# Six result places and shorter rows of scattered transfers in a mixture of experts, and a scan's first decays made one chunk earlier

## The chip, the cores and the metric

The kernel runs on one core of one Trainium2 chip. The metric is device time in microseconds (us), the median of three runs. The profiled execution of the kernel before lasted 853.98 us, of which its instructions span 852.2 us.

## The reference

Two sequences of 1,024 tokens with 128 features go through six residual layers: a small FFN, an attention, the FFN again, a mixture of experts, a bidirectional Mamba-2 layer, and the same mixture of experts again. The change touches the last three.

```python
x = x + 0.5 * ffn(layernorm(x));  x = x + attention(layernorm(x));  x = x + 0.5 * ffn(layernorm(x))
x = x + 0.5 * experts(layernorm(x))      # 8 experts, top 2, at most 320 tokens of a sequence in each
x = x + mamba_bidirectional(layernorm(x))
x = x + 0.5 * experts(layernorm(x))

def experts(h):                           # per sequence, e in 8 experts
    p = softmax(h @ gate.T); pick 2; keep the first 320 tokens of an expert
    y[e] = (silu(h[e] @ w1[e]) * (h[e] @ w3[e])) @ w2[e]          # 320x128, 128x448, 448x128
    out[token] += p[token, e] * y[e]

def mamba(u):                             # each direction
    z, xBC, dt = split(u @ Wi.T); xBC = silu(conv4(xBC) + b); dt = softplus(dt + bias)
    h = h * exp(dt * A) + dt * x * B;  y = h @ C + D * x          # a scan over 1,024 tokens
    return rmsnorm(y * silu(z)) * norm_w @ Wo.T
```

## The kernel before

**Experts.** A unit is one sequence's one expert: units 0 to 15 are the first layer of experts (HALF = 16), 16 to 31 the second. Rows of x are scattered to memory by expert (`scatter`, an indirect DMA of POOL for 128 rows; a routing has 8 or 16 of them). SP loads a unit's 320 rows (`load`, a ring of three), PE turns them (`turn`), and four chunks of hidden features (FCH = 4) follow: `hidden` on PE, `silu` on ACT, `gating` on DVE. `gating` counts the semaphore `gated`, one per chunk over all units, so gated 91 is chunk 2 of unit 22. PE makes the results, ACT keeps them, PE turns them back, and ACT weighs them (`weigh`) into one of OUT places in SBUF, two or so units later. POOL then sends the place to memory by token (`send`, three indirect DMAs a unit, each followed by its landing on `y_out` of the place). `weigh` waits until the last unit in its place has landed. SENT_AT tells for which unit POOL waits for which count of `gated` before it sends, and so how its transfers lie in time; all of POOL's work is one queue in program order. When a sequence's eight units have landed, SP fetches its rows (`fetch`) and DVE adds them to x (`combine`). `address` on DVE makes a unit's row numbers and weights.

**Where the Mamba layer begins.** Beside units 10 to 15 the first sequence is combined and normalised, turned, its step sizes are made (`steps` on PE, `step_sizes` on DVE, `exp_dt` on ACT), and the first direction is projected (`project`, `take`, `first_tap`, `convolve`).

**Scan.** 32 chunks g of 128 tokens, eight (NC) for each of four units of direction and sequence. For a chunk, PE's `before(g)` makes transposes and a product; ACT's `exps(g)` makes the decays between positions: four Relu (L2124), a copy of `bs` (L2129), and one Exp (L2131); DVE's `front(g)` makes `xdt`, `gm` and, with the decays, `mt`; PE's `outputs(g)` and DVE's `back(g)` end it. Each step g of the loops starts chunk g + 1 ahead: `before(g + 1)`, `exps(g + 1)`, `front(g + 1)`. In step 6 of a unit (GATES_AT) ACT also takes both z pieces of the next unit with Silu and makes the four Silu of its convolved rows (`silu_rows`); only then can PE's `before` of the next unit's first chunk begin. In steps 6 and 7 of the first and third scan unit the normalisations for the layers after stand on the same queues.

## Time and profile before

| | us |
|---|---|
| three runs, median (lowest, highest) | 852.98 (852.75, 858.59) |
| profiled execution, its time | 853.98 |
| span of its instructions | 852.2 |
| FFN and attention, first part | 0 to 320 |
| first experts, units 0 to 15 | 320 to 484 |
| scan | 499 to 690 |
| second experts, units 16 to 31, from the end of the scan | 690 to 852 |

Times in the rows are counted from the first instruction. A line number (L1690) is one of the kernel before. The idle time in brackets is that of the engine before the instruction, with what released it; "remote" is a release that the profile can't put down to one instruction. Matmul ends are modelled, and a few per cent of records can be missing.

### The profile page before, as it was taken

How to read it: one execution, taken by the hardware profiler on the slowest of the kernel's cores; microseconds unless marked ns; L12 is line 12 of the kernel's file. 1: busy time of each engine (PE TensorE's matmuls, PEld its weight loads, DVE VectorE, ACT ScalarE, POOL GpSimd, SP SyncE). 2: the span in 40 equal slices, each digit the busy share in tenths (PEclk: the TensorE clock that was granted, in tenths of full speed). 3: DMA queues.
4: the chain of work that ended last, by engine and by line, in shares of the span. 5: the costliest groups of instructions: out<-in, count | busy, mean ns of one | idle time of the engine just before them, and what ended most of it. 6: DMA issues, size and time to landing. Idle time of an engine off the chain costs nothing. (4 is left out here: it accounts for less than half of the span.)

```text
span 852.2 us, 12981 instructions
## 1 busy us (share of the span) xinstructions
PE 716.2 (84%) x4016; PEld 373.4 (44%) x4016; DVE 496.4 (58%) x1453; ACT 543.8 (64%) x938; POOL 298.8 (35%) x328
## 2 busy tenths in 40 slices
PE   4799999989999997898779886778887768797995
PEld 1432222212222224565446454566566645564654
DVE  6778432204855747743437469798798847332352
ACT  5367997889998983644256684967877615342331
POOL 3090003301000434434323456444562732545342
PEclk9799999999999999999889988998999979998998
DMA  4046934521492211112212042112221311211313
GB/s 130 1 187 161 183 86 81 199 91 60 175 261 82 86 36 50 40 34 50 80 28 55 20 117 56 58 50 60 71 72 52 99 49 56 58 42 47 88 53 89
DMA packets 76410, 70.11 MB, mean 82 GB/s; under 512 B 9687, under 2 KB 60233, under 8 KB 76080
## 3 DMA queue, kind: packets, MB, share of 16 engines
q1 hardware_dynamic: 71024, 60.56, 26.6%
q0 software_dynamic: 5024, 8.54, 3.0%
q8 instruction: 36, 0.59, 0.3%
q14 instruction: 38, 0.31, 0.1%
q10 hardware_dynamic: 288, 0.10, 0.1%
HBM read 41.23 MB, written 29.02 MB: 82 GB/s over the span
## 5 line engine op out<-in xcount | busy, mean ns | idle before, releaser
L687 ACT ACTIVATE attn_p<-attn_ps 128x1024 f32<-128x1024 f32 x256 | 240.7, 1059 | 34.7 <-PE attn_ps L703 20.7
L1665 PE MATMUL ps_main<-moe_xsT,moe_w 128*128 128x320 f32 x384 | 131.0, 469 | 14.6 <-issue 9.1
L703 PE MATMUL attn_ps<-attn_p,attn_v 128*32 128x512 f32 x1024 | 137.5, 608 | 4.2 <-issue 4.0
L1675 ACT ACTIVATE moe_act_h<-ps_main 128x320 f32<-128x320 f32 (+1 forms) x128 | 55.1, 433 | 115.2 <-PE ps_main L1665 60.6
L1690 DVE TENSOR_TENSOR moe_hid<-moe_act_h,ps_main 128x320 f32<-128x320 f32 (+1 forms) x128 | 61.9, 485 | 110.8 <-ACT moe_act_h L1675 51.0
L1559 POOL DMA_INDIRECT moe_slots<-rows,moe_scatter_at x64 | 63.8, 997 | 97.8 <-DVE moe_scatter_at L1548 38.0
L680 PE MATMUL attn_ps<-attn_q_rows,attn_k_rows 64*128 64x512 bf16 x448 | 84.5, 388 | 11.5 <-ACT attn_p L687 7.7
L1665 PEld LDWEIGHTS ps_main<-moe_xsT,moe_w 128*128 128x128 f32 x384 | 70.7, 200 | 49.7 <-issue 29.5
L1695 PE MATMUL ps_main<-moe_hid,moe_w 128*128 128x320 f32 (+1 forms) x256 | 74.9, 458 | 5.1 <-DVE moe_hid L1690 3.7
L680 PEld LDWEIGHTS attn_ps<-attn_q_rows,attn_k_rows 64*128 64x128 bf16 x448 | 20.3, 93 | 134.2 <-ACT attn_p L687 119.6
L1765 POOL DMA_INDIRECT moe_rows<-moe_y,moe_dest x48 | 46.2, 962 | 78.6 <-ACT moe_y L1758 39.7
L2084 DVE SCALAR_TENSOR_TENSOR mb_act<-mb_padded,mb_taps,mb_act 128x1024 f32<-128x1024 f32 x48 | 67.1, 1407 | 2.9 <-ACT mb_act L2075 2.3
L1695 PEld LDWEIGHTS ps_main<-moe_hid,moe_w 128*128 128x128 f32 (+1 forms) x256 | 41.9, 192 | 34.7 <-issue 15.3
L1195 POOL TENSOR_TENSOR x_sb<-x_sb,bout_half 128x1024 f32<-128x1024 f32 (+1 forms) x4 | 7.3, 1837 | 104.7 <-DVE rows L1150 104.7
L2245 POOL TENSOR_TENSOR mb_z<-mb_y_in,mb_z 128x256 f32<-128x256 f32 x24 | 26.3, 1098 | 47.8 <-DVE mb_y_in L2236 33.0
L436 POOL TENSOR_SCALAR attn_parts<-attn_q 128x512 bf16<-128x512 f32 x4 | 2.5, 616 | 114.6 <-DVE attn_q L398 114.6
L2124 ACT ACTIVATE mb_e_seg<-mb_cums,mb_cum_col 128x128 f32<-128x128 f32 x128 | 40.5, 389 | 1.2 <-DMA mb_cums<-mb_cum_kept 1.2
L703 PEld LDWEIGHTS attn_ps<-attn_p,attn_v 128*32 128x32 f32 x1024 | 20.6, 108 | 42.5 <-issue 36.9
L2048 PE MATMUL ps_side<-norm_xT,mb_w_xbc 128*128 128x512 f32 x64 | 33.4, 641 | 5.5 <-DVE mb_ab L2017 5.5
L1765 POOL DMA_INDIRECT moe_rows<-mb_y,moe_dest x24 | 22.9, 955 | 38.8 <-ACT mb_y L1758 24.8
L2179 PE MATMUL ps_main<-mb_xw,mb_bs 128*128 128x256 f32 x56 | 20.0, 442 | 19.6 <-DVE mb_h L2202 12.8
L2156 DVE TENSOR_TENSOR mb_mt<-mb_e_seg,mb_gm 128x512 f32<-128x512 f32 x32 | 26.9, 840 | 15.6 <-ACT mb_e_seg L2131 9.5
(273 smaller groups left out, 1288.0 us busy)
## 6 DMA issues: line engine op xcount, KB each, us to landing
mb_cums<-mb_cum_kept SPq DMA_DIRECT2D x32, 256.0 KB
moe_slots<-zeros SPq DMA_DIRECT2D x4, 1380.0 KB, 14.0
attn_q_rows<-attn_q_parts SPq DMA_DIRECT2D x36, 128.0 KB
attn_k_rows<-attn_k_parts SPq DMA_DIRECT2D x36, 128.0 KB
moe_w<-in_w SPq DMA_DIRECT2D x3, 1536.0 KB, 11.6
moe_rows<-zeros SPq DMA_DIRECT2D x4, 1024.0 KB, 16.2
moe_back<-moe_rows SPq DMA_DIRECT2D x16, 256.0 KB, 4.0
mb_e_cum<-mb_e_cum_kept SPq DMA_DIRECT2D x56, 64.0 KB
```

The lines of the kernel that those rows point to most:

```text
L680: ins = self.core.nc.tensor.matmul(into, self.k_rows[rows, ring, pair, keys], self.q_rows[rows, ring, pair, queries], start=True, stop=True)
L687: self.core.nc.scalar.activation(self.p[:, w % self.PB, :, :].rearrange("p a n -> p (a n)"), self.ps_s[:, w % self.SB, :, :].rearrange("p ...
L703: ins = self.core.nc.tensor.matmul(self.ps_av[32 * i:32 * i + 32, :], self.v[:, b * TPB + kt, HGROUPS * i + m, :], self.p[:, w % self.PB, ...
L1559: nc.gpsimd.indirect_dma_start(self.slots[r], bass.IndirectOffsetOnAxis(self.scatter_at[:, b, k, j:j + 1], 0), self.row_of[:, b * TPB + j, ...
L1665: self.core.nc.tensor.matmul(ps[:, w % 2, 0:CAP], wt[:, e, c * P:(c + 1) * P], self.xsT[:, u % 2, :], start=True, stop=True).then_inc(self ...
L1675: self.core.nc.scalar.activation(self.act_h[into, w % 2, :], self.ps_h1[rows, w % 2, 0:CAP], ACT.Silu).then_inc(self.silu_done, 1)
L1690: self.core.nc.vector.tensor_tensor(self.hid[rows, u % 2, c, :], self.act_h[rows, w % 2, :], bank[rows, w % 2, 0:CAP], ALU.mult)\
L1695: return self.core.nc.tensor.matmul(self.y_bank(u)[:, 0:CAP], self.w2[rows, u % E_, c, :], self.hid[rows, u % 2, c, :], start=start, stop= ...
L1765: self.core.nc.gpsimd.indirect_dma_start(self.rows[u // E_], bass.IndirectOffsetOnAxis(self.dest[0:n, u % self.DEST, s:s + 1], 0), self.y[ ...
L2048: self.core.nc.tensor.matmul(bank[:], weight, self.xT[:, t0:t0 + BANK], start=True, stop=True).then_inc(self.proj_done, 1)
L2084: ins = self.core.nc.vector.scalar_tensor_tensor(out, src, tap, out, ALU.mult, ALU.add)
L2124: ins = nc.scalar.activation(self.e_seg[:, g % 2, hh, :], self.cums[:, g % 2, hh, :], ACT.Relu, bias=self.cum[:, di, n, hh:hh + 1], scale= ...
```

## The change

Six things are changed; the renaming of semaphores (`chain` and `sent` become one `addressed`, `dt_exp` and `a_exped` one `exped`) pays for two more `y_out`.

- OUT is 6 in place of 4: places 4 and 5 are lent from tiles of the scan (`y2`'s second part and `y_in`). At the start of the scan `back(0)` and `back(1)` on DVE and the third step of ACT wait for the landing of the units in these places.
- POOL's order in the first experts: the second routing is no longer scattered in one row of eight between units 1 and 2, but in two rows of four between units 3 and 4, which wait for gated 25 and 29. Units 2 and 3 are sent ahead of it without a wait; units 4 and 6 wait for 33 and 37 (they waited for 33 and 38).
- POOL's order in the second experts: both routings in rows of four, the last three of which wait for gated 79, 83 and 86; then five rows of six, two units each, that wait for 91, 96, 101, 106 and 111 (before: two rows of eight, and waits at 87, 94 and 99, the rest sent as soon as weighed).
- The first sequence's `combine`, normalisation, `steps`, `step_sizes`, `exp_dt` and `sums` beside units 10 to 13 stand two chunks to one unit later; `project` 0 and its `take` move from the end of unit 11 into unit 12.
- `exps` is split into `lower`, `keep_b` and `exp_lowered`. For the first chunk of scan units 1 to 3, `lower` and `exp_lowered` run one step earlier on ACT: in step 6, behind `exps` of the last chunk, and ahead of the z pieces and `silu_rows`.
- At the end, `add_last` of a half stands behind `combine` of the same half, not behind both.

```diff
-    OUT, DEST = 4, 8
+    OUT, DEST = 6, 8
...
-        SENT_AT = {2: FCH * 6 + 5, 4: FCH * 8 + 1, 6: FCH * 9 + 2,
-                   HALF: FCH * (HALF + 5) + 3, HALF + 2: FCH * (HALF + 7) + 2, HALF + 4: FCH * (HALF + 8) + 3}
+        SENT_AT = {4: 33, 6: 37, HALF: FCH * HALF + 27, HALF + 2: FCH * HALF + 32, HALF + 4: FCH * HALF + 37, HALF + 6: FCH * HALF + 42, HALF + 8: FCH * HALF + 47}
...
                 for u in range(HALF):
-                    if u == 2:
-                        moe.scatter(pool, 2)
+                    if u == 4:
+                        for n in (0, 4):
+                            pool.wait_ge(moe.gated, FCH * 6 + 1 + n)
+                            moe.scatter(pool, 2, n, n + 4)
                     if u in SENT_AT:
                         pool.wait_ge(moe.gated, SENT_AT[u])
                     moe.send(pool, u)
...
                     if u == HALF:
-                        moe.scatter(pool, 4)
-                        pool.wait_ge(moe.gated, FCH * (HALF + 3) + 2)
-                        moe.scatter(pool, 5)
+                        moe.scatter(pool, 4, 0, 4)
+                        for q, n, at in ((4, 4, 15), (5, 0, 19), (5, 4, 22)):
+                            pool.wait_ge(moe.gated, FCH * HALF + at)
+                            moe.scatter(pool, q, n, n + 4)
...
     def exps(self, act, g):
+        ahead = g >= self.NC and g % self.NC == 0
+        if not ahead:
+            self.lower(act, g)
+        self.keep_b(act, g)
+        if not ahead:
+            self.exp_lowered(act, g)
...
                     if g + 1 < N:
                         mamba.exps(act, g + 1)
+                    if u + 1 < UNITS and i == NC - 2:
+                        mamba.lower(act, g + 2)
+                        mamba.exp_lowered(act, g + 2)
...
-                        if u == 10 and c in (1, 2):
-                            moe.combine(dve, ch, 0, c - 1)
-                            norm.stats_of(dve, ch, c + 15)
+                        if (u, c) in ((10, 3), (11, 0)):
+                            moe.combine(dve, ch, 0, u - 10)
+                            norm.stats_of(dve, ch, u + 6)
...
-                        if u == 11 and c == 3:
+                        if u == 12 and c == 1:
                             mamba.exp_dt(act, 0)
+                        if u == 12 and c == 2:
+                            mamba.take(act, 0, 0)
+                            mamba.first_tap(act, 0, 0)
...
                 for half in range(2):
                     moe.combine(dve, ch, 3, half)
-                for half in range(2):
                     moe.add_last(dve, half)
```

## Rows read from the trace of the kernel before

**Rows 1.** Table by stretch: stretch, its us, busy us by engine, clock, DMA.

```profile
core 0: us, PE busy (x) PEld busy (x) DVE busy (x) ACT busy (x) POOL busy (x), PEclk, DMA share, GB/s
...
499.00:690.00 191.00, 149.79 (x1002) 113.06 (x999) 163.81 (x386) 137.81 (x306) 106.91 (x121) 0.94 0.24 67
...
716.00:852.00 136.00, 112.89 (x467) 72.19 (x465) 50.40 (x159) 46.22 (x123) 59.09 (x61) 0.94 0.24 66
```

**Rows 2.** Order of time, DVE: first gating of units 18, 20, 22, 24, 26.

```profile
716.48 0.49 DVE L1690 TENSOR_TENSOR moe_hid<-moe_act_h,ps_main 128x320 f32<-128x320 f32 x1 [0.69 <-PE ps_main L1665]
...
735.98 0.49 DVE L1690 TENSOR_TENSOR moe_hid<-moe_act_h,ps_main 128x320 f32<-128x320 f32 x1
...
751.55 0.49 DVE L1690 TENSOR_TENSOR moe_hid<-moe_act_h,ps_main 128x320 f32<-128x320 f32 x1
...
765.74 0.49 DVE L1690 TENSOR_TENSOR moe_hid<-moe_act_h,ps_main 128x320 f32<-128x320 f32 x1
...
787.73 0.49 DVE L1690 TENSOR_TENSOR moe_hid<-moe_act_h,ps_main 128x320 f32<-128x320 f32 x1 [0.90 <-PE ps_main L1665]
```

**Rows 3.** Order of time, POOL, second experts: indirect transfers, ends of four rows.

```profile
718.82 0.99 POOL L1559 DMA_INDIRECT moe_slots<-rows,moe_scatter_at  x1 [27.50 <-DVE moe_scatter_at L1548]
...
727.76 0.97 POOL L1559 DMA_INDIRECT moe_slots<-rows,moe_scatter_at  x1 [0.30 <-issue]
...
761.51 0.97 POOL L1765 DMA_INDIRECT moe_rows<-mb_y,moe_dest  x1 [3.84 <-DVE moe_hid L1690]
...
769.97 0.97 POOL L1765 DMA_INDIRECT moe_rows<-moe_y,moe_dest  x1 [1.21 <-issue]
...
780.06 0.91 POOL L1765 DMA_INDIRECT moe_rows<-mb_y,moe_dest  x1 [0.30 <-issue]
```

**Rows 4.** Waits by pair from 300 us on: us in total, times, longest.

```profile
ACT moe_act_h L1675 <- remote: 15.5, 3, 6.4
```

**Rows 5.** Order of time, PE and ACT, unit 19.

```profile
726.93 1.78 PE L1695 MATMUL ps_main<-moe_hid,moe_w 128*128 128x320 f32 x6
...
730.26 0.44 ACT L1675 ACTIVATE moe_act_h<-ps_main 128x320 f32<-128x320 f32 x1 [5.24 <-remote]
```

**Rows 6.** Order of time, POOL, first experts: starts of two rows of transfers.

```profile
399.56 0.97 POOL L1765 DMA_INDIRECT moe_rows<-moe_y,moe_dest  x1 [6.24 <-DVE moe_hid L1690]
...
429.82 0.97 POOL L1765 DMA_INDIRECT moe_rows<-moe_y,moe_dest  x1 [15.44 <-ACT moe_y L1758]
```

**Rows 7.** Order of time, DVE, units 9 and 11.

```profile
410.92 0.49 DVE L1603 COPY moe_xsT<-ps_main 128x320 f32<-128x320 f32 x1 [5.82 <-remote]
...
438.59 0.23 DVE L2015 TENSOR_TENSOR mb_v<-ps_side,mb_dt_bias 128x64 f32<-128x64 f32 x1 [4.48 <-remote]
```

**Rows 8.** Order of time, ACT, scan steps 6 and 7.

```profile
537.29 4.26 ACT L2091 ACTIVATE mb_act<-mb_act,mb_conv_b 128x1024 f32<-128x1024 f32 x4
...
542.71 1.27 ACT L2124 ACTIVATE mb_e_seg<-mb_cums,mb_cum_col 128x128 f32<-128x128 f32 x4
...
544.15 1.28 ACT L2131 ACT_TABLE_LOAD   x1
545.45 0.63 ACT L2131 ACTIVATE mb_e_seg<-mb_e_seg 128x512 f32<-128x512 f32 x1
```

**Rows 9.** Order of time, DVE, at the ends of the three scan units.

```profile
546.11 0.69 DVE L2156 TENSOR_TENSOR mb_mt<-mb_e_seg,mb_gm 128x512 f32<-128x512 f32 x1 [3.06 <-ACT mb_e_seg L2131]
...
549.23 0.70 DVE L2156 TENSOR_TENSOR mb_mt<-mb_e_seg,mb_gm 128x512 f32<-128x512 f32 x1 [1.11 <-ACT mb_e_seg L2131]
...
599.76 0.69 DVE L2156 TENSOR_TENSOR mb_mt<-mb_e_seg,mb_gm 128x512 f32<-128x512 f32 x1 [3.19 <-ACT mb_e_seg L2131]
...
643.55 0.18 DVE L1144 RECIPROCAL norm_rstd<-norm_std 128x4 f32<-128x4 f32 x1 [1.01 <-ACT norm_std L1115]
```

**Rows 10.** Order of time, SP: the fetch of the third sequence's rows.

```profile
790.86 2.01 SPq L1779 DMA_DIRECT2D moe_back<-moe_rows  x4
```

**Rows 11.** Order of time, DVE, the end.

```profile
845.94 0.69 DVE L1786 TENSOR_TENSOR x_sb<-x_sb,moe_back 128x512 f32<-128x512 f32 x1 [0.37 <-DMA moe_back<-moe_rows]
...
847.49 1.48 DVE L1649 TENSOR_TENSOR x_sb<-x_sb,ps_side 128x512 f32<-128x512 f32 x2
```

More of the change, by code:

```diff
@@ L1439, in open @@
         self.act_h, self.hid = sb("act_h", [P, 2, CAP]), sb("hid", [P, 2, FCH, CAP])
-        own = sb("y", [P, self.OUT // 2, 3, D])
-        self.y = [own[:, i, :, :] for i in range(self.OUT // 2)]
+        own = sb("y", [P, 2, 3, D])
+        self.y = [own[:, i, :, :] for i in range(2)]
         self.second = sb("second", [P, 2, 3])
@@ L1449, in open, with landed_of @@
         self.y_kept, self.y_turned = sem("y_kept"), sem("y_turned")
-        self.chain = sem("chain")
+        self.addressed = sem("addressed")
         self.y_out = [sem(f"y_out{i}") for i in range(self.OUT)]
         self.back_in = [sem(f"back_in{i}") for i in range(2)]
-        (self.turned, self.t_read, self.h_done, self.silu_done, self.gated, self.y_done, self.y_read, self.sent, self.combined) = (
-            sem(n) for n in ("turned", "t_read", "h_done", "silu_done", "gated", "y_done", "y_read", "sent", "combined"))
-    OUT, DEST = 4, 8
+        (self.turned, self.t_read, self.h_done, self.silu_done, self.gated, self.y_done, self.y_read, self.combined) = (
+            sem(n) for n in ("turned", "t_read", "h_done", "silu_done", "gated", "y_done", "y_read", "combined"))
+    OUT, DEST = 6, 8
+    def landed_of(self, place, unit):
+        return 48 * len([u for u in range(min(unit, self.LAST)) if u % self.OUT == place])
     UNITS = 2 * B * E_
@@ L2387, in _ @@
                             moe.counts(pe, 2)
-                        if u == 11 and c == 1:
+                        if u == 11 and c == 3:
                             norm.turn(pe, 16)
                             norm.turn(pe, 17)
-                        if u == 13 and c == 0:
+                        if u == 12 and c == 0:
+                            pe.wait_ge(norm.ready, 18)
+                            mamba.steps(pe, 0)
+                        if u == 12 and c == 1:
+                            mamba.project(pe, 0, 0)
+                        if u == 13 and c == 2:
                             mamba.sums(pe, 0)
```

77 lines of the change are left out of this document (40 added, 37 removed).

## The prediction

> **What bounds the kernel now.** I began with the table by stretch, since the change touches three stages with different limits. In the second experts PE is busy for 112.89 of 136.00 us while DVE, ACT and POOL are each under half; in the scan DVE leads with 163.81 of 191.00, ACT follows with 137.81. The granted clock is 0.94 in both, near the upper level, 2.4 GHz [rows 1]. So the experts can win only where PE stands still, and the scan where DVE or its supplier ACT does.
>
> To see whether PE stands still I went to DVE's order of time and read the first `gating` of every second unit. The pairs take 735.98 - 716.48 = 19.50, then 15.57, 14.19 and 21.99 us for the same work [rows 2]. The pair of 14.19 is the plain one; the others are 5.31, 1.38 and 7.80 longer.
>
> What lies beside the long pairs shows in POOL's order of time. Transfers of 0.97 with 0.30 of issue between them stand in rows without a break: eight from 718.82 to 728.73, six from 761.51, and, only 1.21 after these, nine from 769.97 to 780.97 [rows 3]. The plain pair holds the start of the row of six; the worst pair holds the nine that follow it. The list of waits then says what was late: ACT's `silu` waited three times, 15.5 in all and up to 6.4, for a release that the profile can't put to an instruction [rows 4]. One place shows it: PE's matmuls of unit 19 end at 728.71, no later work of PE is needed, and ACT starts at 730.26 after 5.24 idle [rows 5]. The eight transfers ended at 728.73. I read this as PE's progress reaching the others late while a long row runs. In the first experts the same view gives a row that begins at 399.56, and one at 429.82 [rows 6], and DVE stood still for 5.82 and 4.48 inside them [rows 7]. That rows and stalls belong together is a coincidence seen five times, not a proof: the row of eight before 751.55 cost at most 1.38, and the six at 761.51 nothing.
>
> In the scan, ACT's and DVE's orders of time around a change of unit are read together: ACT makes `silu_rows` (four of 4.26), Relu (four of 1.27), loads a table (1.28) and makes Exp (0.63) [rows 8]; DVE's `mt` waits for that Exp, 3.06 and 3.19 at the first two changes, and 1.11 for the next chunk's [rows 9].
>
> **The second experts.** Six places alone remove nothing that I can find: no long wait of `weigh` for a landing is seen, so what they allow is later and shorter rows. First what there is to remove: 1.38 of the second pair and 7.80 of the fourth go in whole. Of the first pair's 5.31, ACT's idle after PE's end is 1.55 and the rest is also routing work, so its stall lies between 1.55 and 5.31; I take 3.6, near the middle. Sum 12.8 (10.7 to 14.5) [rows 2, 5].
>
> What the new rows cost: three rows of four at 79, 83 and 86 behind a first one, and five of six at gated 91, 96, 101, 106 and 111. A chunk of the plain pair takes 14.19 / 8 = 1.77, so five take 8.87; six transfers take 6 x 1.27 = 7.6. A gap of 1.2 to 1.3 is left. A row of six cost nothing at 761.51; the row of six at 429.82 has 4.48 of waiting in it [rows 3, 6, 7]. So five rows cost 0 to 22; I take 1 each, near the row of the same stage, and nothing for rows of four, shorter than any that stalled. Gain 12.8 - 5 = 7.8.
>
> The later sends have a cost behind them: units 22 and 23 wait for gated 106, the second chunk of unit 26, and `fetch` of their sequence stands on SP ahead of the `load` of a later unit. It was issued at 790.86 and took 2.01 [rows 10]. With units some 8 us earlier and the fetch hardly so, the load may be late by 0 to 2.01; I take 0.6, since the ring holds three units. Net -7.2.
>
> The Trainium skill speaks against this. The page "DMA: Bandwidth & Descriptors", in "Issuing engines are not separate DMA queues", says that transfers started by different engines run on the same 16 DMA engines and interleave, so who starts them matters little. By that the same transfers at other times would cost the same, and the 7.8 would be none; the idle of 5.24 does not decide it, as it shows a delay and not its carrier [rows 5].
>
> **The first experts.** The row at 399.56 (twelve transfers) stays, with its waits one count apart. `steps` and `exp_dt` move away from the row at 429.82, where DVE's `step_sizes` had waited 4.48 [rows 6, 7]. Their instructions are the same and stand one chunk to one unit later, with PE's `project` behind them. This saves 0 to 4.48; I take 3.7, since the idle belongs to the wait and units go on beside it. Against this, sends 2 and 3 and the second routing in two fours become nearly one row of fourteen, where before a shorter one did: the nearest prices are 1.38 for eight and 5.82 for twelve, from which I take 1.7 (0 to 5.82), as the fours wait for counts. The `load` of unit 8 has its scatter later, and waits if that lands after unit 7; its margin is small, and its price is inside this range. Net -2.0 (-4.5 to +5.8). The two new waits for places at the start of the scan are for units 10 and 11, sent ahead of 14 and 15, for which the kernel waits there already: nothing.
>
> **The scan.** Three changes of unit. What moves: four Relu (1.27) and one Exp (0.63) of the next unit's first chunk, 1.9 of ACT, from behind `silu_rows` to ahead of it. No instruction and no table load is saved: after the Silu, the next Exp, now that of the second chunk, must load 1.28 [rows 8]. So it is a reordering on an engine that is busy without a break over the change. What wins: `mt` of the first chunk needn't wait for Exp, 3.06 and 3.19 [rows 9]. What loses: the z pieces and `silu_rows` come 1.9 later, so PE's `before` of that chunk, which needs them, comes 1.9 later, and DVE's `gm` behind that. ACT then waits for PE with `keep_b`, where before it made Relu and Exp; behind it in ACT's queue stand the second chunk's Relu and Exp, for whose predecessor DVE waited already (1.11). At the third change DVE waits for a normalisation's root (1.01), which stands behind the moved work, too. Each change can lose 1.9 + 1.28 = 3.2 and gain up to 3.2. I take +2.5, +0.5 and +2.5, nearer the loss, since the shared supplier ACT has no slack there; the second change is the one without normalisations beside it. Sum +5.5 (-3 to +9.6).
>
> The page "ScalarE: Activation LUTs" of the Trainium skill, in "What ACT_TABLE_LOAD costs", adds a drain of about 1.38 us to each load. By it a load exposed at three places would cost up to 4.1 more; in the rows here Exp follows its load within 0.02 us, so I leave it out.
>
> **The tail.** `add_last` of the first half moves ahead of `combine` of the second, which had waited 0.37 for its data; two `add_last` took 1.48 [rows 11]. One of them, 0.74, leaves the end as far as that wait covers it, and the first half is stored sooner: -0.5 (0 to -0.74).
>
> **The sum.** -7.2 - 2.0 + 5.5 - 0.5 = -4.2, from the profiled 853.98: 849.8. That execution is 1.0 above the median of the runs, 852.98; so 848.8, told as 848.5.
>
> **The rivals.** *Rows free, scan free* (838). If no row of six stalls, the second experts give 12.8 - 0.6 = 12.2; if ACT's order gives as much as it takes, the scan gives 0. With -2.0 and -0.5 this is 853.98 - 14.7 - 1.0 = 838.3. For it: the row of six at 761.51 cost nothing, and DVE's waits for Exp are long [rows 2, 3, 9]. Against it: 4.48 beside another row of six [rows 7].
>
> *Gaps too short* (slower, 861). If 1.2 us between rows doesn't let PE's progress through, the five rows of six are one row of thirty. The fifteen transfers from 761.51 to 780.97, parted by 1.21, cost 7.80, 0.52 each [rows 2, 3]: thirty cost 15.6 in place of 12.8, +2.8. With 0.6 for the fetch, the first experts at 0, +5.5 and -0.5 this is 853.98 + 8.4 - 1.0 = 861.4. It decides at the break that ends a row: above 1.2 us my forecast holds. For it: exactly such a break stood ahead of the worst pair. Against: its second row had nine.
>
> *No effect of rows* (858). The change doesn't do what it says: the stalls come with the traffic, which is the same, and not with how it is cut. Then the experts stay, and +5.5 - 0.5 is left: 853.98 + 5.0 - 1.0 = 858. For it: two rows of eight cost so differently. This is where the rule on the 16 engines would lead, too.
>
> **How the numbers follow.** The forecast has 0.50; by its terms' bounds its own range is 843 to 854, and a sixth of it, 0.08, lies below 844.5. Rows and scan free: 0.27. Gaps too short: 0.13, of which half is above 861.5. No effect of rows: 0.10. One per cent of 853, 8.5 us, is about what a measurement of this kernel can tell from no change. Faster by more than that (below 844.5): 0.27 + 0.08 = 0.35; slower (above 861.5): 0.06; the rest, 0.59. The range leaves out the lower third of the free case, 0.09, and some two thirds of the slow one, 0.09: 837 to 860.
>
> **What would show it.** Second experts: pairs of units near 14.2 to 16, no row of POOL above six, ACT's remote waits well under 15.5 in sum. If gaps are too short, the pairs from gated 91 on are near 18, with remote waits at ends of rows of six. First experts: no remote wait of 4 before `step_sizes`; the row at about 400 still stalls. Scan: `mt` of a first chunk without a wait for Exp, but `silu_rows` and PE's `before` 1.9 later, a table load ahead of the second chunk's Exp, and the scan 191 + 5.5 long. If it is 191 or shorter, the loss of ACT's order was wrong; if a row of six has a stall of 4, so was its price of 1.

## The result

The changed kernel takes 873.56 us (median of four runs, 871.1 to 881.02) against 852.87 of the kernel before: 1.0224 times, with a 95% interval of 1.0177 to 1.027. It is slower by some 20 us, outside the range of the prediction. Measured again later, the same pair gave 1.0243 (1.0188 to 1.0298). Ratios are of fast runs alone, slow ones left out, so a ratio can differ from that of two medians. The profiled execution of the changed kernel spans 879.2 us, 27.0 more than that of before.

Both kernels cut at the same points, the first `gating` of units 0, 15, 16 and 31 and the first and last `y_in` of the scan, show where the 27.0 lie:

| stage, us | before | after | difference |
|---|---|---|---|
| up to unit 0 | 329.9 | 329.0 | -0.9 |
| first experts, unit 0 to 15 | 144.2 | 153.3 | +9.0 |
| unit 15 to the scan | 25.1 | 24.4 | -0.6 |
| scan, first to last `y_in` | 187.7 | 199.3 | +11.6 |
| scan to unit 16 | 12.2 | 10.4 | -1.7 |
| second experts, unit 16 to 31 | 129.8 | 138.7 | +8.9 |
| from unit 31 on | 23.3 | 24.1 | +0.8 |

All three changed stages lost in this execution. It is the slowest of the four, 7.5 above their median. In a second profiled one (`after_again`, span 867.5) the scan lost 9.6 and the first experts 6.7, but the second experts 0.6 only. So the first two losses are of the kernel, and the third is mostly of this one execution. The table by stretch of the changed kernel, for the scan and the second experts, answers to [rows 1] (stretch, its us, busy us by engine, clock, DMA):

```profile
core 0: us, PE busy (x) PEld busy (x) DVE busy (x) ACT busy (x) POOL busy (x), PEclk, DMA share, GB/s
507.00:706.00 199.00, 159.19 (x996) 119.22 (x994) 162.24 (x376) 138.01 (x305) 105.97 (x119) 0.89 0.21 63
732.00:879.00 147.00, 124.72 (x474) 79.43 (x473) 53.04 (x181) 47.01 (x125) 59.19 (x61) 0.88 0.21 61
```

DVE, ACT and POOL are busy for as long as before. PE is busy longer, with the same matmuls, and its clock fell from 0.94 to 0.89 and 0.88: more of the time is at the lower of its two levels, 1.2 GHz. So the loss is waiting, and matmuls at half speed beside the waits.

**Second experts.** DVE's order of time, the first `gating` of units 18, 20, 22, 24 and 26, as in [rows 2], with the first of unit 25 and the other three of unit 26:

```profile
736.41 0.49 DVE L1696 TENSOR_TENSOR moe_hid<-moe_act_h,ps_main 128x320 f32<-128x320 f32 x1 [1.87 <-PE ps_main L1671]
...
755.12 0.49 DVE L1696 TENSOR_TENSOR moe_hid<-moe_act_h,ps_main 128x320 f32<-128x320 f32 x1
...
770.99 0.49 DVE L1696 TENSOR_TENSOR moe_hid<-moe_act_h,ps_main 128x320 f32<-128x320 f32 x1
...
788.52 0.49 DVE L1696 TENSOR_TENSOR moe_hid<-moe_act_h,ps_main 128x320 f32<-128x320 f32 x1 [0.55 <-PE ps_main L1671]
...
797.64 0.49 DVE L1696 TENSOR_TENSOR moe_hid<-moe_act_h,ps_main 128x320 f32<-128x320 f32 x1 [1.77 <-ACT moe_act_h L1681]
...
802.89 0.49 DVE L1696 TENSOR_TENSOR moe_hid<-moe_act_h,ps_main 128x320 f32<-128x320 f32 x1
804.12 0.49 DVE L1696 TENSOR_TENSOR moe_hid<-moe_act_h,ps_main 128x320 f32<-128x320 f32 x1 [0.74 <-ACT moe_act_h L1681]
806.16 0.49 DVE L1696 TENSOR_TENSOR moe_hid<-moe_act_h,ps_main 128x320 f32<-128x320 f32 x1 [1.15 <-PE ps_main L1671]
816.48 0.49 DVE L1696 TENSOR_TENSOR moe_hid<-moe_act_h,ps_main 64x320 f32<-64x320 f32 x1 [9.83 <-ACT moe_act_h L1681]
```

The pairs take 18.71, 15.87, 17.53 and 14.37. The bad place has moved: in unit 26 there are 10.32 between two gatings that are neighbours (806.16 and 816.48). POOL's order of time, as [rows 3], says why:

```profile
798.90 0.97 POOL L1771 DMA_INDIRECT moe_rows<-mb_y,moe_dest  x1 [3.25 <-DVE moe_hid L1696]
...
805.23 0.91 POOL L1771 DMA_INDIRECT moe_rows<-mb_y_old,moe_dest  x1 [0.30 <-issue]
806.45 0.97 POOL L1771 DMA_INDIRECT moe_rows<-mb_y,moe_dest  x1 [0.30 <-issue]
...
812.77 0.91 POOL L1771 DMA_INDIRECT moe_rows<-mb_y_in,moe_dest  x1 [0.30 <-issue]
```

The row of six for gated 101 begins at 798.90. The counts 101 and 106 came 6.48 apart (the gatings of 797.64 and 804.12), in less than the 7.6 that six transfers take. So the next six followed with no break: a row of twelve. ACT's order of time, and under it the list of waits, which answer to [rows 5] and [rows 4]:

```profile
816.02 0.43 ACT L1681 ACTIVATE moe_act_h<-ps_main 64x320 f32<-64x320 f32 x1 [7.34 <-remote]
```

```profile
ACT moe_act_h L1681 <- remote: 23.2, 3, 11.2
```

`silu` waits 7.34 for a release that can't be named, and goes on 2.3 after the row's last transfer has ended. From 300 us on these waits add up to 23.2, where they were 15.5; the longest, 11.2, lies beside the row of twelve of the first experts.

**First experts.** POOL's, then DVE's, ACT's and PE's order of time, units 6 to 9, beside [rows 6, 7]:

```profile
371.51 0.97 POOL L1771 DMA_INDIRECT moe_rows<-mb_y,moe_dest  x1 [10.09 <-ACT mb_y L1764]
...
376.22 0.97 POOL L1771 DMA_INDIRECT moe_rows<-mb_y_old,moe_dest  x1 [1.25 <-ACT mb_y_old L1764]
...
385.38 0.97 POOL L1565 DMA_INDIRECT moe_slots<-rows,moe_scatter_at  x1 [0.58 <-issue]
...
389.20 0.97 POOL L1565 DMA_INDIRECT moe_slots<-rows,moe_scatter_at  x1 [0.30 <-issue]
...
405.21 0.97 POOL L1771 DMA_INDIRECT moe_rows<-mb_y,moe_dest  x1 [15.04 <-DVE moe_hid L1696]
```

```profile
387.77 0.49 DVE L1696 TENSOR_TENSOR moe_hid<-moe_act_h,ps_main 128x320 f32<-128x320 f32 x1 [3.17 <-remote]
...
420.25 0.49 DVE L1609 COPY moe_xsT<-ps_main 128x320 f32<-128x320 f32 x1 [8.54 <-remote]
```

```profile
391.97 0.43 ACT L1734 COPY mb_e_seg<-ps_main 128x320 f32<-128x320 f32 x1 [5.97 <-remote]
...
399.23 0.43 ACT L1734 COPY mb_mt<-ps_main 128x320 f32<-128x320 f32 x1 [5.29 <-PE ps_main L1701]
```

```profile
394.50 4.69 PE L1701 MATMUL ps_main<-moe_hid,moe_w 64*128 64x320 f32 x8 [4.91 <-DVE moe_hid L1696]
```

The sends of units 2 and 3 and the eight scatters are fourteen transfers from 371.51 to 390.2, with one break of 1.25. The waits for counts between them make no break: the gatings that the two fours wait for had begun at 376.71 and 384.12, and the second four starts at 385.38 after 0.58. ACT waits 5.97 for a remote release that comes 1.8 after the last of them, and then 5.29 for PE. The row of twelve behind (405.21) costs 8.54 where it had cost 5.82. Unit 7 takes 19.8 in place of 13.5, unit 9 15.5 in place of 12.8. Unit 11, with the later step sizes, takes 9.4 in place of 15.4, but units 12 and 13 5.6 more together.

**Scan.** The first change of unit: ACT's order of time, then DVE's, answering to [rows 8, 9]:

```profile
542.74 1.26 ACT L2140 ACTIVATE mb_e_seg<-mb_cums,mb_cum_col 128x128 f32<-128x128 f32 x4
544.03 0.63 ACT L2151 ACTIVATE mb_e_seg<-mb_e_seg 128x512 f32<-128x512 f32 x1
...
546.95 4.25 ACT L2097 ACTIVATE mb_act<-mb_act,mb_conv_b 128x1024 f32<-128x1024 f32 x4
...
556.44 1.08 ACT L1165 COPY norm_xT<-ps_side 128x512 f32<-128x512 f32 x2 [3.05 <-PE ps_side L1158]
557.40 1.28 ACT L2140 ACTIVATE mb_e_seg<-mb_cums,mb_cum_col 128x128 f32<-128x128 f32 x4
...
558.85 1.28 ACT L2151 ACT_TABLE_LOAD   x1
560.15 0.63 ACT L2151 ACTIVATE mb_e_seg<-mb_e_seg 128x512 f32<-128x512 f32 x1
```

```profile
552.41 0.42 DVE L2169 TENSOR_TENSOR mb_xdt<-ps_main,mb_dt 128x256 f32<-128x256 f32 x1 [2.07 <-PE ps_main L2113]
...
553.13 1.00 DVE L2176 TENSOR_TENSOR mb_mt<-mb_e_seg,mb_gm 128x512 f32<-128x512 f32 x1
...
560.81 0.69 DVE L2176 TENSOR_TENSOR mb_mt<-mb_e_seg,mb_gm 128x512 f32<-128x512 f32 x1 [2.87 <-ACT mb_e_seg L2151]
```

The wait of 3.06 ahead of the first chunk's `mt` is gone (553.13). It has come back in three pieces: 2.07 for PE's `before`, which is behind `silu_rows`; ACT's 3.05 for the normalisation's turn, which PE has behind that; and, since ACT's next work is the second chunk's Relu, table load and Exp, 2.87 for the second `mt`. PE's clock, by stretches of 5 us around `silu_rows`:

```profile
542.00:547.00 5.00, 3.28 (x18) 2.65 (x18) 4.83 (x10) 4.93 (x11) 3.65 (x3) 0.52 0.40 129
547.00:552.00 5.00, 4.15 (x8) 1.54 (x8) 3.27 (x9) 5.00 (x7) 0.72 (x1) 0.50 0.01 3
552.00:557.00 5.00, 5.00 (x32) 4.45 (x32) 2.46 (x5) 1.73 (x6) 1.25 (x3) 0.62 0.00 2
```

The lower level is granted for nearly 14 us, through `silu_rows` and the `before`, outputs and turn behind it. In the kernel before `silu_rows` starts 9.66 sooner; the stretches shifted by as much are:

```profile
532.34:537.34 5.00, 2.81 (x21) 2.35 (x22) 4.89 (x8) 4.94 (x9) 3.26 (x3) 1.00 0.15 49
537.34:542.34 5.00, 2.35 (x11) 1.12 (x10) 4.83 (x15) 5.00 (x7) 1.22 (x3) 1.00 0.09 33
542.34:547.34 5.00, 5.00 (x34) 4.33 (x32) 1.91 (x6) 4.97 (x13) 1.03 (x2) 0.66 0.15 52
```

So the third stretch was partly at the lower level before, too; what is new lies ahead of it. Further on, in chunk 10, the clock has a price. PE's order of time there, after and then before:

```profile
572.17 1.39 PE L2054 MATMUL ps_side<-norm_xT,mb_w_xbc 128*128 128x512 f32 x2 [2.33 <-DVE mb_ab L2023]
...
573.64 1.20 PE L2231 MATMUL ps_main<-mb_act,moe_hid 128*128 128x128 f32 x4
```

```profile
560.71 1.12 PE L2048 MATMUL ps_side<-norm_xT,mb_w_xbc 128*128 128x512 f32 x2 [1.74 <-DVE mb_ab L2017]
...
561.81 0.69 PE L2211 MATMUL ps_main<-mb_act,moe_hid 128*128 128x128 f32 x4
```

### The profile page after: what moved, and what is told of

It is laid out like the page before. It is cut to its first block and busy times, and to the rows that moved or that the text cites. A ratio compares the mean times of both kernels' runs of the same rounds, so it can differ in the third digit from the quotient of the medians.

```text
span 879.2 us, 12988 instructions
## 1 busy us (share of the span) xinstructions
PE 741.6 (84%) x4016; PEld 390.4 (44%) x4016; DVE 497.5 (57%) x1453; ACT 545.0 (62%) x938; POOL 300.7 (34%) x328
## 3 DMA queue, kind: packets, MB, share of 16 engines
q1 hardware_dynamic: 71024, 60.56, 24.4%
q0 software_dynamic: 5024, 8.54, 3.0%
## 5 line engine op out<-in xcount | busy, mean ns | idle before, releaser
L1671 PE MATMUL ps_main<-moe_xsT,moe_w 128*128 128x320 f32 x384 | 138.4, 490 | 22.5 <-DVE moe_hid L1696 18.9
L1671 PEld LDWEIGHTS ps_main<-moe_xsT,moe_w 128*128 128x128 f32 x384 | 74.2, 210 | 58.2 <-issue 39.7
L1565 POOL DMA_INDIRECT moe_slots<-rows,moe_scatter_at x64 | 63.6, 993 | 101.5 <-issue 30.7
L1701 PE MATMUL ps_main<-moe_hid,moe_w 128*128 128x320 f32 (+1 forms) x256 | 80.1, 482 | 7.1 <-DVE moe_hid L1696 7.1
L1701 PEld LDWEIGHTS ps_main<-moe_hid,moe_w 128*128 128x128 f32 (+1 forms) x256 | 44.5, 203 | 39.2 <-issue 17.8
L1771 POOL DMA_INDIRECT moe_rows<-mb_y,moe_dest x30 | 30.4, 1014 | 71.7 <-ACT mb_y L1764 43.8
L1771 POOL DMA_INDIRECT moe_rows<-moe_y,moe_dest x33 | 31.8, 965 | 52.3 <-issue 18.0
L2199 PE MATMUL ps_main<-mb_xw,mb_bs 128*128 128x256 f32 x56 | 19.9, 441 | 18.4 <-DVE mb_h L2222 13.6
L1609 DVE COPY moe_xsT<-ps_main 128x320 f32<-128x320 f32 x32 | 15.6, 487 | 33.2 <-PE ps_main L1599 20.5
## 6 DMA issues: line engine op xcount, KB each, us to landing
moe_slots<-zeros SPq DMA_DIRECT2D x4, 1380.0 KB, 12.7
```

The source lines that it names most:

```text
L1565: nc.gpsimd.indirect_dma_start(self.slots[r], bass.IndirectOffsetOnAxis(self.scatter_at[:, b, k, j:j + 1], 0), self.row_of[:, b * TPB + j, ...
L1671: self.core.nc.tensor.matmul(ps[:, w % 2, 0:CAP], wt[:, e, c * P:(c + 1) * P], self.xsT[:, u % 2, :], start=True, stop=True).then_inc(self ...
L1701: return self.core.nc.tensor.matmul(self.y_bank(u)[:, 0:CAP], self.w2[rows, u % E_, c, :], self.hid[rows, u % 2, c, :], start=start, stop= ...
L1771: self.core.nc.gpsimd.indirect_dma_start(self.rows[u // E_], bass.IndirectOffsetOnAxis(self.dest[0:n, u % self.DEST, s:s + 1], 0), self.y[ ...
```

## The experiments

Ratios are to runs of the kernel before on the same chip, with 95% intervals. Since single runs of one kernel lie some 1% apart, the stages of the profiled execution are often sharper than the ratio. All stage times below are cut as in the first table; each is of one profiled execution, those of the kernel before too.

**The scan's change alone.** The kernel before, with `exps` split and this in ACT's loop:

```diff
                     if g + 1 < N:
                         mamba.exps(act, g + 1)
+                    if u + 1 < UNITS and i == NC - 2:
+                        mamba.lower(act, g + 2)
+                        mamba.exp_lowered(act, g + 2)
```

> The kernel before with nothing but the scan's change: Relu and Exp of a unit's first chunk made one step earlier on ACT. Theory (the loss in the scan is this reordering alone): the scan, 187.7 us from the first to the last y_in in the kernel before and 199.3 in the changed one, is about 199 here, the experts keep their time, and the total is about 11 above the kernel before, 864 (861 to 866). Rival (the scan lost time because lent places and a later start disturbed it, and the reordering by itself costs the 5.5 forecast or nothing): scan 187 to 193, total 853 to 858.

Measured: 866.35 median against 857.51, ratio 1.0067 (1.0029 to 1.0106), scan 200.5. In twelve traces with `exps` in one piece the scan took 187.0 to 190.8; in the three with the change as made it took 197.2 (the changed kernel again), 199.3 and 200.5. The loss of the scan is this reordering alone. By the means of these traces it is 10.3; by the ratio it is 5.7 (2.5 to 9.1), and why the two differ is not shown.

**All but the scan's change.** The changed kernel without those lines.

> The changed kernel with exps again in one piece, all else as changed. Theory (the parts add up): the experts' rows cost 9 in each of the two expert stages, the scan goes back to about 188, total 873.6 - 11 = 862 (859 to 866). Rival (the expert stages' loss is only the poor luck of the one profiled execution, and the scan carries nearly all): 853 to 857. Forecast's own theory (rows of four and six are a gain): 843 to 849.

Measured: ratio 1.0061 (1.0027 to 1.0095), 862.68 median, scan 189.1, first experts 150.9, second experts 124.6. The scan goes back, the first experts keep their loss. The second experts didn't: 124.6 here and 138.7 in the changed kernel are the same order of POOL, and so the stalls there vary by many us from run to run.

**The same decays, placed behind `silu_rows`.**

```diff
                             mamba.silu_rows(act, u + 1)
                             mamba.take(act, u + 1, 5)
+                            mamba.lower(act, g + 2)
+                            mamba.exp_lowered(act, g + 2)
                             mamba.square(act, g - 1)
```

> The kernel before with the scan's change at another place: the first chunk's Relu and Exp are still made in step 6, but behind silu_rows and the z pieces. Theory (the loss comes from the 1.9 put ahead of silu_rows, which holds up PE's before and all that is queued behind it on PE, and leaves ACT without work while it waits): scan back to 188 to 190, total as the kernel before within 3. Rival (any early making of the first chunk's decays costs, for instance by its table load or its place in the e_seg ring): scan 195 or more.

Measured: scan 194.7, ratio 1.0114 (1.0077 to 1.0152), by the time no better than `ahead_only`. Neither theory in full. The first change of unit lost 0.4 only: chunks 7 to 10 took 6.3, 4.3, 6.1 and 7.2 (6.7, 3.5, 6.1 and 7.2 before). At the second and third, 3.0 and 4.1 were lost. PE's and DVE's order of time at the second:

```profile
591.69 0.33 PE L2110 MATMUL ps_main<-ident,mb_act 128*128 128x128 f32 x1 [1.47 <-ACT mb_bs L2139]
592.89 1.17 PE L2191 MATMUL ps_main<-mb_xw,mb_bs 128*128 128x256 f32 x2 [0.87 <-issue]
593.86 3.11 PE L2048 MATMUL ps_side<-norm_xT,mb_w_xbc 128*128 128x512 f32 x4
```

```profile
598.28 0.42 DVE L2250 COPY mb_y_in<-ps_main 128x256 f32<-128x256 f32 x1 [3.41 <-PE ps_main L2233]
```

PE's `before` of the second chunk waits 1.47 for the copy of the first chunk's `bs`, which on ACT now stands behind its Exp; before, it stood ahead of the table load and Exp. After two short waits PE is at half speed (3.11 for four matmuls that take 1.88 at the upper level), and DVE waits 3.41 for it. So the 1.9 ahead of `silu_rows` was the cause at the first change, but it is not the only wrong place: here Exp stands ahead of a copy that PE waits for, and PE's clock falls, too.

**The second experts' order alone.** Six places, the new rows of the second experts and the tail; no change in the scan and none in the first experts.

> Six places and the changed order of POOL in the second experts (rows of four, five rows of six) and the tail; first experts and scan as before. Theory (rows merge when five chunks go by faster than six transfers take, and a merged row stalls as a long one does): no gain, 852 to 858, with a row of twelve in it and an idle of 5 or more at its end. Rival (the rows do what was forecast, and only what came ahead of them, the clock and the first experts, spoiled it): 843 to 848, no row above six or eight.

Measured: ratio 1.0022 (0.9983 to 1.006), second experts 131.0. No row was above eight here, so twelve was not the rule. The one of eight, from 732.9 to 743.0, is two rows of four run together, as in every trace with this order: again the count had come before POOL did. And beside four of the five rows of six ACT and DVE stood idle together for 3.0 to 3.9, by both engines' orders of time (in the plain pair of before, 2.0 at most), though the breaks ahead of these four rows were 2.3 to 5.8. With the new rows the second experts took 138.7, 130.4, 131.0 and 124.6 (mean 131.2); with the old ones, in six traces, 127.5 to 136.4 (mean 131.9). No effect. In one place the new order lost: in two of its four traces, this one and `after_again`, unit 28 takes 12.1 and 13.4, where it takes 7.4 in all six of the old order. SP issues the load of unit 29 only behind the fetch of the third sequence. In `after_again` the fetch comes at 810.2, in unit 27 (before: 790.86, in unit 26), and PE waits for the rows of unit 29, and then runs at half speed; PE's order of time:

```profile
817.53 0.99 PE L1599 MATMUL ps_main<-ident,moe_xs 128*128 128x128 f32 x3 [2.95 <-DMA moe_xs<-moe_slots]
818.45 2.50 PE L1671 MATMUL ps_main<-moe_xsT,moe_w 128*128 128x320 f32 x4
```

**The first experts' change, whole and in halves.** `order1_only` has both halves, `overlap_only` the later places of `combine`, `steps` and what goes with them, `pool1_only` POOL's order (sends 2 and 3 first, then two fours, then sends 4 to 7). All three have six places, with second experts and scan as before.

> Six places and the changed order of POOL and of the first sequence's steps in the first experts; second experts and scan as before. Theory (sends of units 2 and 3 and the scatter of the second routing, put next to each other, are one row of fourteen from 371 to 390 and cost more than the step sizes gain): first gating of unit 0 to that of unit 15 about 153 in place of 144, total 858 to 864. Rival (the forecast's: step sizes gain 3.7, the rows cost 1.7): 849 to 853.

Measured: ratio 1.0038 (1.0003 to 1.0073), first experts 150.8: the theory's way, if 2 less than its 153.

> Six places, and in the first experts only the later places of the first sequence's combine, normalisation, steps, step sizes and first projection; all of POOL's orders as in the kernel before. Theory (this half of the first experts' change is not what loses): unit 11 is 5 or more shorter than 15.4, units 12 and 13 get 5 back together, first gating of unit 0 to that of unit 15 between 141 and 146, total within 3 of the kernel before. Rival (the loss of 6.5 in the first experts is this move): 149 to 153 there and 5 longer in total.

Measured: ratio 0.9983 (0.995 to 1.0016), first experts 142.7; unit 11 takes 9.1, units 12 and 13 5.6 more. A gain of 1.5 against the one trace of the kernel before, none that the time can show, and none against other traces: with the old places of these steps, unit 11 takes 15.4 in `before`, `rows2_only` and `pool1_only`, but 10.5 in `ahead_only`, `ahead_behind` and `thin_sends`. So the stall that was to be removed is not always there, and where it is not, units 11 to 13 take 30.7, 4 less than with the new places (34.9).

> Six places, and in the first experts only POOL's changed order: units 2 and 3 sent at once, the second routing in two fours between units 3 and 4, then units 4 to 7. Theory (this order is the loss: eleven transfers in one row end late, PE stands still and its clock falls): unit 7 takes about 19.8 in place of 13.5 and unit 9 about 15 in place of 12.8, units 0 to 15 take 150 to 153, total 5 to 7 above the kernel before. Rival (it is the other half): unit 7 13.5, total as before.

Measured: ratio 1.0114 (1.0062 to 1.0166), first experts 151.2, unit 7 19.8, unit 9 13.6. POOL's order is the loss, and most of it stands in unit 7, at 19.7 to 19.9 in every trace that has it (13.4 to 13.6 with the old order). The five such traces take 150.8 to 153.3 for the first experts (mean 151.4), four with both halves as before 139.2 to 144.6 (mean 142.2): 9.2.

**Bytes or rows.** The sends of the kernel before at an eighth of their bytes; seven eighths of the results are left out.

```diff
-indirect_dma_start(self.rows[u // E_], ...
-                   self.y[u % self.OUT][0:n, s, :], ...
+indirect_dma_start(self.rows[u // E_].rearrange("r (a c) -> (r a) c", c=16), ...
+                   self.y[u % self.OUT][0:n, s, 0:16], ...
```

> The kernel before with each sent row of results cut from 512 to 64 bytes: as many transfers, rows and waits on POOL, an eighth of the bytes of the sends; seven eighths of the experts' results are left out. Theory A (the stalls come with the length of a row of POOL's transfers, not with its bytes): the idle of about 4 to 6 near the row of twelve in unit 9 stays, and unit 9 takes 12 or more. Theory B (they come with the traffic): unit 9 takes 8 or less, the idle is gone, and the total falls by 5 to 15.

Measured: ratio 0.9976 (0.9935 to 1.0017); unit 9 takes 12.7, with an idle of 4.4 beside the row of twelve. The bytes of the sends are not the cause of this stall. Whether they add to those of the second experts is open: units 20 to 27 take 61.2 here, and 65.3 to 69.9 in the six traces of the same order with whole rows.

**Breaks.** `overlap_only` with a wait ahead of each send:

```diff
     def send(self, pool, u):
         pool.wait_ge(self.y_read, 3 * (u + 1))
         pool.wait_ge(self.addressed, 3 * (u + 1))
+        if u % (2 * E_) != 0:
+            pool.wait_ge(self.y_out[(u - 1) % self.OUT], self.landed_of((u - 1) % self.OUT, u))
```

> overlap_only with one thing more: POOL sends a unit's three transfers only when those of the unit before it have landed, so that no row of sends is longer than three and a landing lies between rows. Theory (the stalls belong to long rows without a break): the idle of 4 to 6 beside the twelve transfers near 400 us is gone, unit 9 takes 8 to 9 in place of 13, the second experts lose the idles beside sends and keep those beside the two rows of eight scatters; 5 to 9 below overlap_only. Rival (a stall comes with a transfer or its landing, however it is parted): idles only move, the time is that of overlap_only within 2, or longer, since the last rows of a sequence land some 8 us later.

Measured: ratio 1.0035 (1.0002 to 1.0069). The stall is gone where it was largest. POOL's order of time, the starts of the rows of units 4 to 7:

```profile
396.59 0.97 POOL L1773 DMA_INDIRECT moe_rows<-mb_y,moe_dest  x1 [4.57 <-DVE moe_hid L1696]
...
402.05 0.97 POOL L1773 DMA_INDIRECT moe_rows<-mb_y_in,moe_dest  x1 [1.99 <-ACT moe_y L1764]
...
407.57 0.97 POOL L1773 DMA_INDIRECT moe_rows<-moe_y,moe_dest  x1 [2.05 <-DVE moe_hid L1696]
...
412.95 0.97 POOL L1773 DMA_INDIRECT moe_rows<-moe_y,moe_dest  x1 [1.91 <-DMA moe_rows<-moe_y,moe_dest]
```

With some 2 us between threes, unit 9 takes 6.0 where it took 13.1 in `overlap_only`, with the same transfers and bytes. ACT's remote waits fell from 11.1 for `silu` to none (2.4 are left, before a copy). The gain was paid back: the first sequence's last row ends at 416.4, 3.8 later than in `overlap_only`, while unit 10 begins 8.3 sooner, so DVE waits 7.75 there for the fetched rows, and the unit takes 17.6 (11.0 in `overlap_only`); unit 28, behind the fetch of the third sequence, takes 15.6.

The rows of scatters broken, too:

```diff
+            if q in (2, 4, 5) and n in (3, 6):
+                pool.wait_ge(self.scattered[b], 16 * (self.spread_out[b] - 1))
             nc.gpsimd.indirect_dma_start(self.slots[r], ...
```

> landed_sends, and the rows of eight scatters of routings 2, 4 and 5 in three, three and two, each behind the landing of the ones ahead. Theory (long rows): units 18 to 21 take 30 to 31 in place of 35, so 3 to 4 below landed_sends. Rival (the idle there is routing work and not the row): no change, or 2 to 4 longer where the first load of a sequence waits for its scatter.

Measured: ratio 1.002 (0.9986 to 1.0053). Units 18 to 21 take 30.7 in place of 35.0, the second experts 124.4 in place of 132.7 in all; unit 7, whose scatter lands later, 15.1 in place of 13.4, and unit 28 16.0; the tail takes 1.6 more. No remote wait is left in the list.

**The changed kernel again**, beside these two.

> The changed kernel once more, word for word, beside the same runs of the kernel before as the other two, so that its parts can be set against the whole. The parts measured so far are a median of 9 longer for the scan (ahead_only), 10 for POOL's order in the first experts (pool1_only), 2 shorter for the later steps (overlap_only) and none for the second experts' rows (rows2_only). Theory (the parts add): ratio 1.015 to 1.023. Rival (the parts act on each other, as a late part moves all of POOL's rows): above 1.025 or below 1.012.

Measured: 871.58 median, ratio 1.0243 (1.0188 to 1.0298). This lies between the theory's range and the rival's. The four parts' ratios less one, 0.0067 + 0.0114 - 0.0017 + 0.0022, make 1.0186, just below the interval. But `order1_only` in place of its two halves makes 1.0127, and `ahead_only` with `no_ahead` 1.0128, some 10 us short. By the means of the traces the scan lost 10.3, the first experts 9.2, and the second experts won 0.7, 18.8 together of the 20.7. So the places are shown; by the ratios it is open whether the parts simply add.

**Breaks, and what they made late.** `landed_all` without counts ahead of sends, the first sequence's `combine` and the steps behind it one chunk later, and the third fetch on SP behind the load of unit 29.

> landed_all with what its breaks made late put right: no counts to wait for ahead of sends (a unit is sent as soon as it is weighed and the one before it has landed), the first sequence's combine and the steps behind it one chunk later, and the fetch of the third sequence on SP behind the load of unit 29 in place of ahead of it. Theory (breaks take the stalls away, and what ate their gain in landed_all was the wait for the last landing of a sequence, 17.6 for unit 10 and 16.0 for unit 28): unit 10 takes 10 to 13, unit 28 under 11, total 843 to 848, ratio to the kernel before 0.985 to 0.993. Rival (the rows' gain can't be kept, since three transfers and a landing take 5.4 and stretch every sequence's last landing): 852 to 856, ratio within 0.003 of 1.

Measured: ratio 1.0046 (1.0016 to 1.0076). The theory was half wrong. The second experts take 117.2, 12.6 less than before, each unit from 19 to 28 between 6.8 and 7.4. But the tail takes 31.2, 7.9 more: POOL sends one unit every 5.4 at best, every 5.9 on the whole from 754.40 on, and is behind at the end, the last row starting at 837.09, 15 after unit 31 began. And the first experts take 146.2, since units 11 and 12 now wait (17.0 and 16.7), and unit 15 to the scan 4.3 more.

**Breaks in the second experts alone.** `overlap_only` with each routing's scatters in two fours, the second behind the landing of the first; the sends behind the landing of the last scatter, without counts; and those of units 17 to 25 behind the landing of the unit before:

```diff
+            if q in (4, 5) and n == 4:
+                pool.wait_ge(self.scattered[b], 16 * (self.spread_out[b] - 1))
...
+        if 2 * E_ < u < 3 * E_ + 2:
+            pool.wait_ge(self.y_out[(u - 1) % self.OUT], self.landed_of((u - 1) % self.OUT, u))
...
-        SENT_AT = {2: ..., 4: ..., 6: ..., HALF: FCH * (HALF + 5) + 3, HALF + 2: ..., HALF + 4: ...}
+        SENT_AT = {2: FCH * 6 + 5, 4: FCH * 8 + 1, 6: FCH * 9 + 2}
...
-                    if u in (E_ + 3, HALF + E_ + 4):
+                    if u in (E_ + 3, HALF + E_ + 5):
...
                         moe.scatter(pool, 5)
+                        pool.wait_ge(moe.scattered[1], 16 * moe.spread_out[1])
```

> overlap_only (six places, later steps in the first experts, no change in the scan), with breaks in the second experts alone: scatters in fours, each behind the landing of the last four; units 17 to 25 sent when the unit before has landed, the rest as soon as weighed; the fetch of the third sequence on SP one unit later. Theory (the 12.6 by which the second experts fell from 129.8 to 117.2 in the kernel with breaks everywhere were the stalls, and the tail's 8 came from POOL being full with its waits for landings): second experts 118 to 123, tail 23 to 27, ratio to the kernel before 0.985 to 0.993. Rival (POOL's whole queue of 61 transfers is the bound, and what the stalls give back stands in the tail whatever is waited for): stage and tail together 148 to 153 as in the kernel before, ratio 0.995 to 1.003.

Measured: 848.38 median against 856.63, ratio 0.9907 (0.9868 to 0.9946); second experts 123.8, 0.8 above the theory's range, tail 23.0; the ratio is the theory's.

And with that condition `u > 2 * E_`, so that the sends up to the last wait for the landing ahead:

> The same, but every unit of the second experts from 17 on waits for the landing of the one before. Theory: second experts as in breaks2_early, 117 to 121, and a tail 3 to 6 longer, since the last sends still come one landing after the other. Rival: the two are alike, as the last rows are paced by weighing and not by landings.

Measured: 847.2 median, ratio 0.9852 (0.9794 to 0.9909); second experts 122.8, tail 24.0. The two are alike within their intervals, as the rival said of them: with fewer breaks among the scatters, the sends start 47.0 and 45.9 after unit 16 in place of 49.6 (`breaks`), and POOL is no longer behind at the end. Both are faster than the kernel before, and so than the changed one. Not all is won: the second four of one routing and the first of the next still run together, eight in a row, and units 18 and 19 take 20.8, where they take 16.4 in `breaks`; that the row is the cause was not tested. The table by stretch of the last one, over most of its second experts, and under it that of the kernel before:

```profile
716.00:826.00 110.00, 103.91 (x407) 65.22 (x406) 45.67 (x150) 43.69 (x115) 56.01 (x58) 0.95 0.23 66
716.00:826.00 110.00, 96.14 (x378) 60.37 (x377) 42.69 (x143) 40.38 (x106) 53.38 (x55) 0.95 0.23 65
```

PE is busy for 94% of it, where it was for 87%.

## Why the prediction was wrong

**What bounds the kernel**: right. PE standing still in the experts, and DVE waiting for ACT in the scan, are where the time went.

**The second experts, -7.2: the price of the new rows failed.** That 12.8 of stalls were there to remove is as good as shown: with breaks everywhere the stage fell by 12.6, and the three pairs by 3.1, 1.4 and 7.7, where 3.6, 1.38 and 7.80 were told. What failed is "five rows cost 0 to 22; I take 1 each". Units 20 to 27, where these rows lie, take 56.8 with breaks (`breaks`) and 66.1 in the kernel before. With rows of six they take 63.3, 65.2, 65.4 and, in the profiled changed kernel, 71.5: five rows cost 6.5 to 14.7, about as much as the rows they replace (9.3). In that one execution two of them ran together. "Nothing for rows of four" failed, too, as two of these ran together each time: units 18 to 21 take 31.5 to 34.6 with them, and 30.6 in `breaks`. The rival "gaps too short" had this mechanism: a count of chunks doesn't make a break, as five chunks can go by in 6.48. Its point of decision was wrong, though: rows of six stalled with breaks of 2.3 to 5.8 ahead of them, too. It looks as if the length of the row itself decides: beside threes no idle stands out, beside sixes 2.5 to 4.1 at times, eights up to 4.7, twelves 4.4 to 8.5.

**The fetch, 0.6**, was the right mechanism, in two traces of four: the load behind it was late, and unit 28 took 4.7 and 6.0 more, above the bound of 2.01. What the bound left out is in `after_again`'s rows: PE waits 2.95, and the four matmuls behind take 2.50, where four of that kind took 1.24 just ahead. In the other two traces it cost 0.2.

**The first experts, -2.0: the sign failed.** The step was "sends 2 and 3 and the second routing in two fours become nearly one row of fourteen ... from which I take 1.7 (0 to 5.82), as the fours wait for counts". The counts had been reached, so eleven transfers from 376.22 on ran without a break, and the row cost 6.3 in unit 7, just above the bound of 5.82 that the row of twelve had given. What was left out is the clock: PE stands for 4.91 behind that row, and its next eight matmuls take 4.69, where eight of that kind take 2.51 at the upper level (at 384.94). The gain of 3.7 for the later step sizes was taken from one trace: it was a gain of 6 in unit 11, given back in units 12 and 13 but for 1.5, and there is none against the traces in which the stall is missing. The load of unit 8, which I had feared, was no part of it: it was issued at 391.82, and when PE came to its rows at 400.57, it had waited for ACT and not for them.

**The scan, +5.5: the right mechanism, mis-sized.** The path was as told: `silu_rows` 1.9 later, PE behind it, ACT idle for PE, the table load ahead of the second Exp. It measured 11.6, above the upper bound of 9.6 (10.3 by the means). By chunk, 5.3 of it lie at the first change of unit, 2.3 and 2.5 at the next two, where +2.5, +0.5 and +2.5 had been taken, and the rest elsewhere. At the first change, chunks 7 and 8 lose 1.3 and 2.0, together what the sum had as its bound for a change (3.2). Two chunks later, chunk 10 loses 1.6 more, and this is a term the sum didn't have: PE waits 2.33 for DVE, its granted clock is 0.66 from 572 to 577 (1.00 in 560 to 565 of the kernel before), and four matmuls take 1.20 where they took 0.69. The 14 us at the lower level around `silu_rows` are not the price: in the two other traces with the change it is 6.9, with 4.9 and 4.8 lost at the same change.

**The range.** At their bounds, the terms reach from some 830 to some 882; the 843 to 854 that the prediction calls the range by its terms' bounds is narrower, and its lower bound for the scan, -3, has no working, where three changes that gain 3.2 would make -9.6. The measured 873.56 lies inside the wide one.

**The tail** gained nothing that can be seen: it took 0.8 more in one trace, 0.4 less in the other.

**The same transfers at other times, and the table load.** By the page "DMA: Bandwidth & Descriptors" of the Trainium skill, in "Issuing engines are not separate DMA queues", transfers run on the same 16 engines whoever starts them; the prediction drew from it that the same transfers at other times should cost the same. Here they don't: broken by landings, the same transfers take 12.6 less of the second experts, and sends with an eighth of the bytes left the stall in unit 9. The page "ScalarE: Activation LUTs" of the Trainium skill, in "What ACT_TABLE_LOAD costs", has a drain of some 1.38 with each table load; here Exp starts at 560.15, 0.02 after the load from 558.85 ends, so that this was rightly left out.

What stays open: by what way a row of POOL's transfers holds up the other engines' releases. That they come late and shortly after the row is shown; that PE's own progress is what is late was read from the times only. Whether the landing matters or only the 2 us between threes was not parted. The spread of the second experts between runs of one order (124.6 to 138.7) is not explained, either.

## What to carry to other kernels

Look for idle times with no named releaser, and set them beside the rows of indirect transfers: parting such rows into threes by a wait for a landing, where a count of other work had often been reached already, was worth 1 to 1.5% here, as long as the queue that issues them isn't behind at the end. Before work is moved ahead on a busy engine, ask which other engine waits for what stands behind it, and price that engine's matmuls at the lower clock, as a longer wait can bring it. A wait removed in one place was found again one chunk later. And look whether a stall stands in more than one trace before its removal is counted as a gain.

## What the runs showed of the hardware

Beside twelve indirect transfers in a row `silu` waited 7.34 and a copy 8.54 for a release that the profile can't name; cutting the bytes of each send to an eighth left an idle of 4.4 (5.82 before), and 2 us between threes took it away (unit 9 from 13.1 to 6.0). A transfer in a row takes 1.27 of POOL, 0.97 and 0.30, with whole rows as with an eighth of their bytes; from the end of three to the release at their landing it is 1.9 to 2.1. Waits of 1.47 and 0.87 close together were followed by matmuls at half speed (3.11 for 1.88).
